# One order of TensorE's work in every slot of the attention, and P times V four slots behind the scores

## The reference

```python
q = (query @ Wq + bq).reshape(b, s, 16, 32).transpose(0, 2, 1, 3)     # k, v alike, from ctx
scores = jnp.einsum('bhqd,bhkd->bhqk', q, k) / jnp.sqrt(32.)
scores = jnp.where(j < i, scores, -1e30)                               # strictly causal
attn = softmax(scores); attn[:, :, 0, :] = 0
ctx = jnp.einsum('bhqk,bhkd->bhqd', attn, v).transpose(...).reshape(b, s, d)
x = layer_norm(query + ctx @ Wo + bo)
out = layer_norm(x + relu(x @ W1 + b1) @ W2 + b2)
```

## Time and profile before

| what | us |
|---|---|
| median of 3 runs | 2656.3 (2654.1 to 2656.74) |
| profiled execution | 2657.87, its span 2656.1 |
| mean granted TensorE clock | 0.99 of 2.4 GHz |
| PE busy | 2507.3 (94% of the span) |
| DVE, ACT, POOL busy | 2098.6, 1629.0, 1574.0 |

### The profile page before, as it was taken

The page is one execution under the profiler, slowest core; times in us unless marked ns, Lnnn a source line. Parts: engine busy times, 40 slices in busy tenths (PEclk is TensorE's granted clock), DMA queues, the critical chain, the costliest instruction groups (busy, mean ns, idle before and its releaser), DMA issues.

```text
span 2656.1 us, 62863 instructions
## 1 busy us (share of the span) xinstructions
PE 2507.3 (94%) x22664; PEld 1889.3 (71%) x22664; DVE 2098.6 (79%) x4886; ACT 1629.0 (61%) x2881; POOL 1574.0 (59%) x1721
## 2 busy tenths in 40 slices
PE   4899999999999999978999999999999999999998
PEld 1455555555555555557888888888888888888887
DVE  7999999999999999779767677676767676767675
ACT  2788888999999999777343444343434344444433
POOL 2677777777777777656555555454545554454543
PEclk9999999999999999989999999999999999999999
DMA  5444444443343333346131322222222222222220
GB/s 164 113 117 117 116 114 112 113 107 102 96 104 103 105 104 99 86 130 173 49 68 47 68 51 68 53 66 56 61 60 57 65 57 64 57 65 56 65 57 25
DMA packets 444456, 225.04 MB, mean 85 GB/s; under 512 B 302368, under 2 KB 388192, under 8 KB 444144
## 3 DMA queue, kind: packets, MB, share of 16 engines
q1 hardware_dynamic: 442544, 219.71, 32.6%
q10 hardware_dynamic: 1600, 1.31, 0.2%
HBM read 112.36 MB, written 57.69 MB: 64 GB/s over the span
## 4 chain that ended last, share of the span: by engine, by line
PE 59%; POOL 24%; issue 12%; DVE 3%; DMA 1%; SPq 1%; ACT 0%; POOLq 0%; DVEq 0%; ACTq 0%
PE h_ps L1659 25%; POOL prob_lo L495 24%; PE acc L1675 22%; PE front L1645 6%; PE lin_ps L934 2%; PE o_ps L976 1%; PE max_ps L907 1%; PE st_ps L956 1%; PE lin_ps L930 1%; DVE W L1616 1%; POOL scan L510 0%; PE st_ps L991 0%; POOLq L83 0%; PE o_ps L978 0%; SPq L1078 0%
## 5 line engine op out<-in xcount | busy, mean ns | idle before, releaser
L495 POOL TENSOR_TENSOR prob_lo<-probs,prob_hi 128x512 f16<-128x512 f32 (+1 forms) x768 | 792.5, 1039 | 348.2 <-ACT prob_hi L582 314.9
L1659 PE MATMUL h_ps<-x_halves,W 128*128 128x256 f16 x6144 | 754.9, 273 | 3.6 <-ACT hf L1444 3.6
L1675 PE MATMUL acc<-W,hs 128*128 128x256 f16 x5376 | 669.6, 273 | 0.0
L1659 PEld LDWEIGHTS h_ps<-x_halves,W 128*128 128x128 f16 x6144 | 595.9, 98 | 88.4 <-issue 16.0
L1444 ACT ACTIVATE hf<-h_ps,b1s,scale_evac 128x256 f32<-128x256 f32 x512 | 284.6, 562 | 568.6 <-PE h_ps L1659 568.1
L1675 PEld LDWEIGHTS acc<-W,hs 128*128 128x128 f16 x5376 | 526.0, 98 | 60.9
L1369 POOL TENSOR_TENSOR hf<-hf 128x256 f32<-128x256 f32 x256 | 241.2, 942 | 493.4 <-ACT hf L1444 493.1
L588 ACT ACTIVATE probs<-st_ps,exp_scale 128x512 f32<-128x512 f32 (+1 forms) x768 | 467.1, 608 | 104.2 <-PE st_ps L991 84.4
L886 DVE CUSTOM_DVE_ANT_0 max_ps<-max_ps,mask_q 128x256 f32<-128x256 f32 (+2 forms) x768 | 419.1, 561 | 85.4 <-PE max_ps L907 84.6
L582 ACT ACTIVATE prob_hi<-probs 128x512 f16<-128x512 f32 (+1 forms) x768 | 427.3, 556 | 22.4 <-issue 7.2
L1612 DVE TENSOR_TENSOR hs<-hf,hs 128x896 f16<-128x896 f32 x256 | 281.2, 1118 | 143.6 <-ACT hs L1433 143.6
(11 more groups left out here) (152 smaller groups left out, 3540.9 us busy)
## 6 DMA issues: line engine op xcount, KB each, us to landing
heads<-stage SPq DMA_DIRECT2D x748, 64.0 KB, 2.1
raw_c<-in_cT SPq DMA_DIRECT2D x64, 256.0 KB, 3.2
raw_x<-in_xT SPq DMA_DIRECT2D x64, 256.0 KB, 4.4
o_in<-ctx_rows SPq DMA_DIRECT2D x256, 64.0 KB, 2.5
x_in<-in_x SPq DMA_DIRECT2D x32, 512.0 KB, 4.0
x_rows<-x SPq DMA_DIRECT2D x64, 256.0 KB, 2.1
o_in<-x_rows SPq DMA_DIRECT2D x256, 64.0 KB, 2.4
out<-y SPq DMA_DIRECT2D x32, 512.0 KB, 3.0
```

The lines of the kernel that those rows point to most:

```text
L495: pool.tensor_tensor(prob_lo[:, k % 4, 0:w], probs[:, k % PROBS, 0:w], prob_hi[:, k % 4, 0:w], ALU.subtract).then_inc(pl_done, 1)
L1659: last = pe.matmul(h_ps[:, f % 2, 0:T], W1[:, aw, j, f * P:(f + 1) * P], x1_halves[:, item.parity, aa, j, :], start=(j == 0 and m == 0), s ...
L1675: last = pe.matmul(acc_products[:, n, :], hs[:, p % HS, aa, n, :], W2[:, p, aw, n, :], start=(p == 0 and m == 0 and n % 2 == 0), stop=(p = ...
```

## The change

All slots now have one order on TensorE: projections, maxima, scores (which open `st_ps`), mask (which closes it and counts `st_done`), values. The projections and all that follows from them, up to the transposed scores, stand one slot earlier (`LIN` 47), with the loads of x, splits, looks and ranges of the inputs moved along; `PV_AT` = `ST_AT` + 4 keeps the values in the slot in which they stood. The four buffers stay four. The feed part begins one slot earlier.

```diff
-    LOAD = {"c": (0, 1, 2, 3), "x": (3, 6, 9, 12)}
-    LOOK = {"c": (9, 11), "x": (16, 20)}
+    LOAD = {"c": (0, 1, 2, 3), "x": (2, 5, 8, 11)}
+    LOOK = {"c": (8, 10), "x": (15, 19)}
...
-    SPLIT = {"c": 36, "x": 48}
+    SPLIT = {"c": 35, "x": 47}
-    LIN = 48
+    LIN = 47
...
-    PV_AT = ST_AT + 3
+    PV_AT = ST_AT + 4
...
-        def transposed_scores(window, s, opens):
+        def transposed_scores(window, s):
...
-                if opens:
-                    wait_for(pe, exp_done, SLOTS, item, k + 1 - 2)
+                wait_for(pe, exp_done, SLOTS, item, k + 1 - 2)
                 for m, (kt, at) in enumerate(ST_UNITS[c]):
                     w = S - kt * P
-                    last = pe.matmul(..., start=(opens and m == 0), stop=not opens,
-                                     skip_group_check=True)
-                if not opens:
-                    last.then_inc(st_done, 1)
+                    pe.matmul(..., start=(m == 0), stop=False,
+                              skip_group_check=True)
...
-                if s % 2 == 0:
-                    linear(window, s)
-                    maximum_scores(window, s)
-                    transposed_scores(window, s, True)
-                    masks(window, s, False)
-                    values(window, s)
-                else:
-                    values(window, s)
-                    masks(window, s, True)
-                    transposed_scores(window, s, False)
-                    linear(window, s)
-                    maximum_scores(window, s)
+                linear(window, s)
+                maximum_scores(window, s)
+                transposed_scores(window, s)
+                masks(window, s)
+                values(window, s)
...
-FEED_AFTER = 46
+FEED_AFTER = 45
```

More of the change, by code:

```diff
@@ L165, in attention @@
     assert D == S == 512 and HD == 32 and B % 2 == 0 and B > BACK
-    LOAD = {"c": (0, 1, 2, 3), "x": (3, 6, 9, 12)}
-    LOOK = {"c": (9, 11), "x": (16, 20)}
-    TOPS = 21
-    SPREAD = 22
-    GATHER = 26
-    RANGE = 31
-    SPLIT = {"c": 36, "x": 48}
+    LOAD = {"c": (0, 1, 2, 3), "x": (2, 5, 8, 11)}
+    LOOK = {"c": (8, 10), "x": (15, 19)}
+    TOPS = 20
+    SPREAD = 21
+    GATHER = 25
+    RANGE = 30
+    SPLIT = {"c": 35, "x": 47}
     SPLIT_STEP = 3
-    LIN = 48
+    LIN = 47
     OUT = LIN + 4
@@ L951, in transposed_scores @@
                     wait_for(pe, rows_loaded[t % 2], 128, item, 64 * (t // 2 + 1))
-                if opens:
-                    wait_for(pe, exp_done, SLOTS, item, k + 1 - 2)
+                wait_for(pe, exp_done, SLOTS, item, k + 1 - 2)
                 for m, (kt, at) in enumerate(ST_UNITS[c]):
                     w = S - kt * P
-                    last = pe.matmul(st_ps[:, k % 2, at:at + w], heads[t][0:98, 1, i, kt * P:(kt + 1) * P],
-                                     heads[t][0:98, 0, i, kt * P:S], start=(opens and m == 0), stop=not opens,
-                                     skip_group_check=True)
-                if not opens:
-                    last.then_inc(st_done, 1)
+                    pe.matmul(st_ps[:, k % 2, at:at + w], heads[t][0:98, 1, i, kt * P:(kt + 1) * P],
+                              heads[t][0:98, 0, i, kt * P:S], start=(m == 0), stop=False,
+                              skip_group_check=True)
         def values(window, s):
@@ L981, in values, with masks @@
                 last.then_inc(pv_done, 1)
-        def masks(window, s, opens):
+        def masks(window, s):
             for item, k in due(window, s, SLOTS, B, ST_AT, SLOTS):
@@ L988, in masks @@
                 tiles = st_ps[:, k % 2, :].rearrange("p (c n) -> p c n", n=P)[:, 0:KT:unit[-1][1] // P or KT, :]
-                if opens:
-                    wait_for(pe, exp_done, SLOTS, item, k + 1 - 2)
                 last = pe.matmul(tiles, identb[:, :], mask_k[:, 0:len(unit), :] if k % 3 else mask_k0[:, :, :],
-                                 start=opens, stop=not opens, skip_group_check=True)
-                if not opens:
-                    last.then_inc(st_done, 1)
+                                 start=False, stop=True, skip_group_check=True)
+                last.then_inc(st_done, 1)
         for window in range(B + BACK):
             for s in range(SLOTS):
-                if s % 2 == 0:
-                    linear(window, s)
-                    maximum_scores(window, s)
-                    transposed_scores(window, s, True)
-                    masks(window, s, False)
-                    values(window, s)
-                else:
-                    values(window, s)
-                    masks(window, s, True)
-                    transposed_scores(window, s, False)
-                    linear(window, s)
-                    maximum_scores(window, s)
+                linear(window, s)
[3 more added lines that the diff above has]
+                values(window, s)
                 yield
```

## The result

| kernel | median us | lowest to highest | profiled execution | its span | clock |
|---|---|---|---|---|---|
| before, 4 runs | 2656.52 | 2654.1 to 2658.75 | 2657.87 | 2656.1 | 0.990 |
| changed, 4 runs | 2689.13 | 2688.74 to 2689.65 | 2688.74 | 2686.9 | 0.982 |

The changed kernel is slower by 1.27% (ratio 1.0127, 95% interval 1.0115 to 1.014), 33 us. The forecast was 2619 us, 37 us faster, and the range ended at 2648.

What follows compares the result with a forecast made beforehand. In the attention, TensorE, VectorE and ScalarE, near 90% busy, wait on each other through short buffers. 2657.87 - 35 (quarters of the items) - 2 (the end) = 2621 profiled, so 2619 us median; 8 in 10: 2599 to 2648.

Steps and rivals of the forecast that it cites:

- the slower rival: No spare buffer before `prob_hi`: VectorE's lateness passes into ScalarE and on to the scores; 2680 to 2714 us, chance 0.11.
- term 3: Attention, quarter by quarter, with VectorE and ScalarE as bounds: 2.4 us less an early item, 2.3 a late one, 35 us.
- if C and D grow by what A and B lose: Sign of a wrong forecast: an item's third and fourth quarters grow by what its first and second lose.
- The values' distance: TensorE's values: four slots after scores give 2.4 us of slack, so `prob_lo` waits all but go, up to 28.5 us.
- The normalised output: TensorE's wait for it before values becomes part of the maxima's wait: 10.8 us at most, only a part credited.
- given back: Rival: ScalarE and VectorE already bind the last three quarters; 0.5 to 0.8 us an item, 10 us, 2646; chance 0.19.
- The even spacing: Scores on TensorE all 1.30 us apart: costed at nothing, a few tenths per item possible in the upper bound.
- VectorE's table: Same VectorE instructions bunched otherwise, splits now sharing a slot with L807: zero, with 0.3 us an item either way.
- the rule against item 5: VectorE with two SBUF inputs and reading GpSimd exclude each other: 0.3 us per split, gain 2.3 to about 2, sum 2624.
- `prob_hi` behind values k-4: ScalarE's L582 waits for values four units back, no buffer spare: cover 0.4 us, cost nothing unless values are late.
- The end: Last item: one more slot covers 1.3 to 1.4 us of a `prob_lo` stall; -2 us, bounds 0 and -6.

Runs made afterwards that it cites:

- c1_ahead: The changed kernel with the second load of c issued in slot 0, ahead of the heads' transfers, third and fourth one slot up: 2653.74 us, ratio 0.9998.
- order_alone: The changed kernel's one order on TensorE with the table of the kernel before and values three slots behind scores: 2652.65 us, ratio 1.0001.
- before_c1_behind: The kernel before with the second load of c moved from slot 1 to slot 2, behind the heads' transfers: 2663.03 us, ratio 1.0033.
- before_short_looks: The kernel before with VectorE's two looks at c reading 64 of each 1024 columns: 2661.55 us, ratio 1.0038.
- changed_looks_mid: The changed kernel with the looks at c moved to slots 21 and 24, their exchange behind them, loads of c unmoved: 2653.69 us, ratio 0.9993.

## Why the prediction was wrong, point by point

Two steps failed, each by some 35 us: 2619 was forecast, c1_ahead measures 2653.7, the changed kernel 2689.1.

**The first step that failed**, and the reason why the kernel is slower and not only not faster, is a part of the change that the prediction did not work out. It gives the projections' slots as moved and says of the rest "semaphore counts, projections and matmul shapes stay"; nowhere does it go through SyncE's list. The diff showed the line `LOAD = {"c": (0, 1, 2, 3), ...}` with c's numbers unchanged and x's moved, and `GROUP_READY` hangs on `LIN`. That puts 12 transfers, 8.77 us of issuing, ahead of the load that VectorE's first look at c needs. None of the rivals held this mechanism; the slower rival (no spare buffer) gave 2680 to 2714 and so came near the measured 2689 by accident.

**The second step that failed** is term 3, the 35 us of the sum, 2.3 or 2.4 in each item. With the load back in its place (c1_ahead) the six early items together took 0.1 us more than before and the seven late ones 3.1 more. What the prediction named as its sign of being wrong, "if C and D grow by what A and B lose", is what happened: in the early items A and B lost 0.8 us and C and D grew by 0.9. With VectorE relieved by the looks a part came through, 13 and 14 us.

1. *The values' distance* was right: the waits for `prob_lo` went from 28.5 us to no row at all.
2. *The normalised output* was right in direction: 10.8 us (17.1 up to 1190 us) to no row in the changed kernel, 5.2 in c1_ahead. It was late VectorE in another place, as the step said.
3. *What is late next* was right for B (16.2 us forecast and measured) and for A by 0.1 instead of 0.5, and wrong for C, which even with the load ahead rose from 17.9 to 19.3 us in the late items where 17.5 was forecast. The error: C "cannot go under VectorE's 17.32" was taken as a floor for C by itself. VectorE's program is continuous; if B gets shorter on TensorE but not on VectorE (16.9 us in every kernel), C starts on TensorE with VectorE further behind and grows by the difference. A floor has to be put on the whole item at the slowest engine, not on each quarter at its own. The rival "given back" had this; it forecast 10 us faster; c1_ahead's interval runs from 3 us faster to 2 slower. In kind that rival was right for the change without its fault, and even its 10 us were too many.
4. *The even spacing* was worth nothing measurable: order_alone 1.0001.
5. *VectorE's table* was put at zero with 0.3 us an item either way. The durations of VectorE's instructions sum to 77.9 us per late item before, 79.5 in the changed kernel, 79.7 in c1_ahead and 80.1 in order_alone (the records overlap, so the sum is above the item): 1.6 to 2.2 us against the change; in the early items they are 80.5, 80.4, 80.5 and 81.4. The parts: splits and rows, in the groups below. The paragraph with the rule against item 5 had the mechanism, and its sum is wrong: 0.3 us for each of eight splits is 2.4 us an item, which would take all of the 2.3 and not bring it to 2; with 15 x 2.4 = 36 us the time is 2655, next to c1_ahead's 2654.
6. *`prob_hi` behind values k-4* was right for ScalarE: no row in the changed kernel, 2.9 us in one place in c1_ahead. GpSimd has the wait instead: `prob_lo` for TensorE's values 40.8 us, 22.0 before. The slower rival is refuted: c1_ahead has the same four buffers and is not slower.
7. *The end*: the last two items took 121.6 us (119.1 in c1_ahead) for 128.8, where a gain of 2 was forecast, with 6 as the bound. Some 5 us of this looks like chance: before_c1_behind and before_short_looks, whose edits act ahead of this stretch, took 123.8 and 124.4 for it, so the one profiled execution of the kernel before was slow there. Against these the gain is 2 to 5 us.

The groups for step 5, splits and rows in the kernel before, then in the changed one (busy us, mean ns):

```profile
L596 DVE SCALAR_TENSOR_TENSOR acts<-raw_c,inverse,acts 128x512 f16<-128x512 f32 x64 | 58.6, 915 | 0.0
...
L821 DVE SCALAR_TENSOR_TENSOR negmax_parts<-maxima,negmax_parts 128x16 f16<-128x16 f32 x64 | 28.0, 438 | 2.2
...
L819 DVE TENSOR_SCALAR negmax_parts<-maxima 128x16 f16<-128x16 f32 x64 | 16.7, 261 | 0.0
```

```profile
L596 DVE SCALAR_TENSOR_TENSOR acts<-raw_c,inverse,acts 128x512 f16<-128x512 f32 x64 | 74.0, 1157 | 0.0
...
L596 DVE SCALAR_TENSOR_TENSOR acts<-raw_x,inverse,acts 128x512 f16<-128x512 f32 x64 | 61.3, 961 | 0.0
...
L819 DVE TENSOR_SCALAR negmax_parts<-maxima 128x16 f16<-128x16 f32 x64 | 31.0, 484 | 2.1
...
L821 DVE SCALAR_TENSOR_TENSOR negmax_parts<-maxima,negmax_parts 128x16 f16<-128x16 f32 x64 | 13.2, 207 | 2.2
```

The split of c costs 1157 ns for 915, that of x 961 for 1065: the same work beside other instructions of GpSimd. A split that starts when GpSimd has just ended, in the kernel before, and one that starts 0.28 us into GpSimd's `prob_lo`, in the changed one (start, us, what):

```profile
572.27 1.16 POOL L495 TENSOR_TENSOR prob_lo<-probs,prob_hi 128x512 f16<-128x512 f32 x1 [0.41 <-ACT prob_hi L582]
...
573.49 0.75 DVE L596 SCALAR_TENSOR_TENSOR acts<-raw_c,inverse,acts 128x512 f16<-128x512 f32 x1
```

```profile
720.95 1.16 POOL L495 TENSOR_TENSOR prob_lo<-probs,prob_hi 128x512 f16<-128x512 f32 x1 [0.57 <-ACT prob_hi L582]
721.23 1.43 DVE L596 SCALAR_TENSOR_TENSOR acts<-raw_c,inverse,acts 128x512 f16<-128x512 f32 x1
```

The second ends 0.55 us behind GpSimd's instruction, and so do all its kind: 30 splits of c in the changed kernel start with over 0.5 us of GpSimd's instruction left, and each ends 0.55 us behind it; the 20 that meet no GpSimd instruction take 740 ns in the mean. L819 and L821 do the same: they end 0.03 us behind it, and take 170 to 180 ns where it is idle. So VectorE waited for GpSimd's instruction to end, and by the new table the splits of c and L819 start earlier inside one, so that more of it is left to wait for. The Trainium skill (SBUF — State Buffer, "SBUF: two separate sides") has VectorE with two SBUF inputs and a reading GpSimd lock each other out for a whole instruction; for the splits the traces agree with it. That the whole gain would have come without these waits is not shown.

**Left open**: what would free D of the early items, where SyncE stands between GpSimd's blocks (L398, 25.2 us in changed_looks_mid) and the gather (L439, 35.5 us); no version found is faster by clearly more than 0.2%. A version with the heads' transfers spread over two engines wasn't tried.

## What to carry to other kernels

When a table of slots is shifted, go through every engine's program, the one that only issues transfers first of all: write down what now stands ahead of each load and how long its issuing takes, because a load that keeps its slot while its neighbours move has moved too. When engines are near 90% busy, put the floor on a whole period at the slowest engine: TensorE's waits that vanish in one quarter (28.5 us here) came back as waits for VectorE in the next. Count too what the slowest engine's own instructions will cost at their new places: here it was 2.1 us an item, next to a forecast gain of 2.3. And before taking work off the slowest engine, ask what is late behind it: here it was SyncE's list again, at the gather and at the mixed blocks.

## What the runs showed of the hardware that was not expected

- Issuing is dear: twelve transfers of heads took SyncE 8.77 us, 0.6 us each with one of 1.63, and four of rows 2.68. The Trainium skill (DMA: Bandwidth & Descriptors, "Issuing engines are not separate DMA queues") says that the sequencer's time to start a transfer is usually small beside the transfer. Here it isn't: 0.6 us stands beside the 2.1 us in which such a transfer lands, and the issuing ahead of a load that lands in 3.1 us took 8.77.
- One load of 1024 KB landed in 6.4 us (c) and 6.0 (x) where four of 256 KB took 3.1 and 4.4 each: the last quarter of an input is there sooner by four issues than by one, when they are spread over slots.
- Some VectorE instructions (L596, L819, L821) that start inside one of GpSimd's wait for its end: 16 columns took 207 or 438 ns in the mean (L821), and 484 or 261 (L819), by where it stands, and 512 columns 740 ns where GpSimd was idle and up to 1.66 us where it wasn't.
- The mean granted clock fell to 0.92 and 0.85 of 2.4 GHz in single quarters in which TensorE had stood for others for some microseconds, while it read 1.00 in the quarters around.
